# Block 1 attention: zero-padded tail operands, matmuls ordered by shape, five wide mark pairs on VectorE, new beat tables

## The reference, cut to what matters

```python
# two blocks on x of 32 sequences x 256 tokens x 128 features; after each part x = layernorm(x + part(x))
x = ln(x + state_space_mixer(x)); x = ln(x + ffn(x))          # block 0
# block 1, attention with 16 heads of 64, 4 memory keys in front of the 256 keys:
q, k, v = x @ Wq, x @ Wk, x @ Wv            # split by head; mem_k, mem_v put in front of k, v
dots = einsum('bhid,bhjd->bhij', l2norm(q), l2norm(k)) * 10
dots = einsum('hg,bgij->bhij', W_pre_th, dots)        # heads mixed before
dots = where(causal, mask_value, dots)
dots = where(dots < top_k(dots, 64)[0][..., -1:], mask_value, dots)
attn = einsum('hg,bgij->bhij', W_post_th, softmax(dots))   # heads mixed back
out = (attn @ v * head_scale) * sigmoid(x @ Wg + bg) @ Wo
x = ln(x + out); x = ln(x + ffn(x))
```

## Time and profile before

| | us |
|---|---|
| median of 3 runs (lowest, highest) | 4013.77 (4002.79, 4021.79) |
| the profiled execution's own time | 4020.4 |
| its span, first to last instruction | 4019.1 |
| mean granted TensorE clock in it | 0.953 of full |
| PE, DVE, ACT, POOL busy | 3641.7, 3418.9, 3097.5, 2068.1 |

### The profile page before, as it was taken

How to read it: one execution, slowest core, us unless ns; L and a number is a source line. 1 busy time by engine, 2 the same in 40 slices (tenths; PEclk the granted TensorE clock), 3 DMA queues, 4 the chain that set the end, 5 groups by cost and what they waited for, 6 DMA issues and landing times.

```text
span 4019.1 us, 78953 instructions
## 1 busy us (share of the span) xinstructions
PE 3641.7 (91%) x19551; PEld 2621.6 (65%) x19551; DVE 3418.9 (85%) x18221; ACT 3097.5 (77%) x10773; POOL 2068.1 (51%) x3991
## 2 busy tenths in 40 slices
PE   5999999986899998999999999999999999999987
PEld 3888888863666666666666666666666666666665
DVE  6888888835998888998999989988888889898894
ACT  5777777755788888888888888888888888888863
POOL 0000000014666667676666766666666766676664
PEclk7999999996999999999999999999999999999998
DMA  3000000001111111111111111111111111111110
GB/s 120 12 11 12 11 12 11 9 9 35 25 27 27 31 30 31 31 27 27 27 28 27 27 27 30 29 26 27 27 30 31 31 30 28 26 27 28 25 25 4
DMA packets 168123, 106.00 MB, mean 26 GB/s; under 512 B 78000, under 2 KB 165104, under 8 KB 166896
## 3 DMA queue, kind: packets, MB, share of 16 engines
q1 hardware_dynamic: 167664, 100.96, 11.7%
HBM read 20.70 MB, written 8.91 MB: 7 GB/s over the span
## 4 chain that ended last, share of the span: by engine, by line
POOL 29%; PE 27%; ACT 25%; issue 10%; DVE 7%; SPq 1%; DMA 1%; POOLq 0%; DVEq 0%; ACTq 0%
POOL below L1849 10%; PE bank L362 6%; POOL T L1859 6%; ACT T L1494 4%; ACT L1463 4%; POOL below L1851 3%; PE bank L330 3%; PE bank L1335 3%; POOL gate L1870 3%; ACT SN L1507 3%; POOL posts L1811 2%; ACT gate L1549 2%; DVE y L895 2%; PE bank L1356 2%; PE bank L431 1%
## 5 line engine op out<-in xcount | busy, mean ns | idle before, releaser
L1714 DVE MATCH_REPLACE8 W<-last,W 128x130 f32<-128x130 f32 (+17 forms) x3456 | 871.5, 259 | 0.0
L1735 DVE MAX8 last<-W 128x8 f32<-128x130 f32 (+17 forms) x3456 | 761.0, 261 | 0.0
L1849 POOL TENSOR_SCALAR below<-T,last 128x260 f32<-128x260 f32 (+8 forms) x576 | 597.7, 1038 | 176.6 <-DVE last L1733 126.2
L1494 ACT ACTIVATE T<-T,peak 128x260 f32<-128x260 f32 (+15 forms) x1024 | 418.1, 422 | 168.0 <-POOL T L1859 159.0
L1811 POOL TENSOR_SCALAR posts<-post,share 128x128 f32<-128x128 f32 x1024 | 376.2, 387 | 246.1 <-DVE share L1644 239.0
L1325 PE MATMUL bank<-T,pre 128*128 128x40 f32 (+15 forms) x1024 | 377.6, 452 | 126.0 <-ACT T L1515 103.5
L1335 PE MATMUL bank<-posts,T 128*128 128x128 f32 (+7 forms) x2048 | 412.2, 307 | 61.2 <-ACT AT L1532 57.8
L885 DVE TENSOR_TENSOR_SCAN hs<-dA,dx 128x256 f32<-128x256 f32 x512 | 349.5, 683 | 134.0 <-issue 100.7
L1507 ACT ACTIVATE SN<-bank,rq 128x260 f32<-128x260 f32 (+1 forms) x1024 | 360.7, 433 | 98.1 <-DMA T<-SN 46.2
L1335 PEld LDWEIGHTS bank<-posts,T 128*128 128x128 f32 (+7 forms) x2048 | 302.5, 182 | 182.7 <-POOL posts L1811 104.2
L521 POOL TENSOR_SCALAR k_sq<-k_sq 128x16 f32<-128x16 f32 x64 | 19.5, 305 | 707.0 <-DVE k_sq L534 572.4
(11 more groups left out here) (242 smaller groups left out, 9503.1 us busy)
## 6 DMA issues: line engine op xcount, KB each, us to landing
T<-SN SPq DMA_DIRECT2D x32, 130.0 KB
x_in<-in_xT SPq DMA_DIRECT2D x32, 128.0 KB, 2.2
x_mid<-x_b SPq DMA_DIRECT2D x32, 128.0 KB, 1.7
xb<-x_mid SPq DMA_DIRECT2D x32, 128.0 KB, 2.1
out_y<-x_d SPq DMA_DIRECT2D x32, 128.0 KB, 3.4
T<-SN SPq DMA_DIRECT2D x32, 126.0 KB
T<-SN SPq DMA_DIRECT2D x32, 122.0 KB
T<-SN SPq DMA_DIRECT2D x32, 118.0 KB
```

The costliest lines, as they stand in the source:

```text
L1494: act.activation(one, one, ACT.Exp, bias=peak[k % 2][:, j:j + 1], accum_out=total[k % 4][:, j:j + 1]).then_inc(e_made, 1)
L1714: dve.match_replace(both[:, s, at:to], best[n], both[:, s, at:to], LOWEST).then_inc(ranked, 1)
L1735: dve.max(best[n], both[:, s, at:to]).then_inc(ranked, 1)
L1849: pool.tensor_scalar(out[:, s, :], x[:, s, :], best[:, 7:8], DROP, ALU.is_lt, ALU.mult).then_inc(marked, 1)
```

## The change

1. `V2` and `AT2` get 128 partitions instead of 4. `V2` is filled with zeros once, `AT2` as before; data still goes to the first four. The matmuls of the last four tokens in `attend` now have 128 rows instead of 4.
2. `mix_back` does a whole quad at once: it waits for all four `posts`, and issues the matmuls in an order in which those of like shape stand together.
3. `CUT` names the wide pairs of quads 0, 2, 4, 6 and 7. Their marks are written by DVE at the end of `wide`; POOL only adds them. The other four wide pairs (those of quads 1, 3 and 5, and the 132-wide one of quad 7) and the narrow ones stay with POOL.
4. All beat tables have new numbers.

```diff
-    V, V2 = room.sb("V", [P, 2, INNER]), room.sb("V2", [MEM, INNER])
+    V, V2 = room.sb("V", [P, 2, INNER]), room.sb("V2", [P, INNER])
-    AT2 = room.sb("AT2", [MEM, HEADS, QG])
+    AT2 = room.sb("AT2", [P, HEADS, QG])
+    CUT = [[0], [], [0], [], [0], [], [0], [0]]
-    PE_MIX = (64, 71, 87, 94, 107, 110, 119, 123)
+    PE_MIX = (56, 71, 89, 96, 121, 125, 126, 129)
-    DVE_SHARE = (40, 66, 80, 84, 108, 111, 120, 135)
+    DVE_SHARE = (65, 83, 85, 98, 114, 117, 124, 136)
...
-        def mix_back(b, i, j):
+        def mix_back(b, i):
...
-            pe.wait_ge(posts_made, n + 1)
+            pe.wait_ge(posts_made, n + 4)
...
+            order = [(first, 0), (first, 1)]
+            if width(QUAD[i][2]) <= P // 2:
+                order += [(second, 0), (second, 1), (first, 2), (first, 3)]
+            else:
+                order += [(first, 2), (first, 3), (second, 0), (second, 1)]
+            for one, j in order:
+                last = one(j)
...
+            if j0 in CUT[i]:
+                out = mark_of(g, j0)
+                dve.wait_ge(found_wide, 2 * ((QUADS + 1) * b + i + j0 // 2 + 1))
+                if drops(k, DROPS[i][0]) > 1:
+                    dve.wait_ge(dropped, drops(k, DROPS[i][0]) - 1)
+                for n, (j, s) in enumerate(rows):
+                    dve.tensor_scalar(out[:, s, :], x[:, s, :], best[n][:, 7:8], DROP, ALU.is_lt, ALU.mult).then_inc(cut_marked, 1)
+                    yield
...
+                if j0 in CUT[i]:
+                    made.append((x, out, cut_marked, 2 * cuts(k, j0)))
+                    continue
```

More of the change, by code:

```diff
@@ L1147, in rank_steps, with cuts, mark_of @@
         return n
+    def cuts(k, j):
+        b, i = divmod(k, QUADS)
+        return CUT_ALL * b + sum(len(c) for c in CUT[:i]) + sum(x <= j for x in CUT[i])
+    def mark_of(g, j0):
+        return below[j0 // 2][:, 0:2 * width(g)].rearrange("p (two n) -> p two n", two=2)
     def drops(k, j):
@@ L1171, in attention_phase @@
[L1171 to L1185, removed]
@@ L1215, in attention_phase @@
-    ACT_K_SCALE = (13, 34)
-    POOL_K_CLIP = (1, 24)
-    POOL_K_ROOT = (11, 25)
+    PE_K = (-7, -6, 3, 3)
+    PE_K_TURN = (1, 2, 11, 24)
+    PE_Q = (11, 20, 23, 33)
+    PE_Q_SUM = (26, 30, 35, 36)
+    PE_Q_TURN = 44
+    PE_ATTEND = (5, 8, 8, 18)
+    PE_GATES = (34, 37, 39, 40)
+    PE_MIX = (56, 71, 89, 96, 121, 125, 126, 129)
+    PE_OUT = 25
+    PE_VAR1 = 33
+    PE_SPREAD1 = 38
+    PE_W1 = 41
+    PE_W2 = 45
+    PE_H1 = (63, 67, 67, 69)
+    PE_H2 = (79, 80, 91, 93)
+    PE_SCORE0 = (55, 60, 63)
@@ new lines, in attention_phase @@
+    PE_W3 = 94
+    PE_SCORE1 = (89, 91, 93, 95, 96, 100, 105, 107)
+    PE_VAR2 = 98
+    PE_SPREAD2 = 109
+    PE_V = (123, 127, 128, 128)
+    PE_PREMIX = [[71, 83, 89, 93, 104, 105, 118, 123], [125, 125, 128, 131, 136, 148, 164, 197]]
+    ACT_K = (-33, -24, 17, 21)
+    ACT_K_TURN = (9, 27, 30, 38)
+    ACT_Q = (30, 42, 43, 43)
+    ACT_K_ROOT = (-16, 24)
+    ACT_Q_SUM = 48
+    ACT_Q_ROOT = 55
+    ACT_PEAK = (-8, 33, 38, 42, 70, 78, 92, 114)
+    ACT_WIDE = (34, 39, 56, 69, 70, 80, 98, 123)
@@ L1219, in ctx_of @@
+    ACT_K_SCALE = (3, 28)
+    POOL_K_CLIP = (-21, 10)
+    POOL_K_ROOT = (-14, 12)
     def ctx_of(c2):
@@ L1410, in tensor @@
                 for i in range(QUADS):
-                    for j in range(4):
-                        if (b := whose(p, t, PE_MIX[i])) is not None:
-                            mix_back(b, i, j)
+                    if (b := whose(p, t, PE_MIX[i])) is not None:
+                        mix_back(b, i)
                 if (b := whose(p, t, PE_OUT, 2)) is not None:
@@ L1533, in at_keep @@
             if i == 0:
-                act.activation(AT2[:], turn(at1[0:MEM, 2 * P:3 * P]), ACT.Copy).then_inc(at_kept, 1)
+                act.activation(AT2[0:MEM, :, :], turn(at1[0:MEM, 2 * P:3 * P]), ACT.Copy).then_inc(at_kept, 1)
             if i == QUADS - 1:
@@ L1855, in drop @@
                 marks += 2
-                made.append((x, out, marks))
-            for x, out, n in made:
-                pool.wait_ge(marked, n)
+                made.append((x, out, marked, marks))
+            for x, out, ready, n in made:
+                pool.wait_ge(ready, n)
                 pool.tensor_tensor(x, x, out, ALU.add).then_inc(dropped, 1)
```

105 lines of the change are left out of this document (48 added, 57 removed).

## The result

| | before | changed |
|---|---|---|
| time, median | 4017.78 us (4 runs, 4002.79 to 4025.67) | 3849.31 us (4 runs, 3845.96 to 3863.54) |
| ratio, with its 95% interval | | 0.9592 (0.9554 to 0.963) |
| profiled execution, its span | 4020.4, 4019.1 us | 3863.54, 3862.2 us |

The sign was right; the size was not.

The account below looks back on a forecast made before the run. No engine was full; POOL's latency was what was waited for. DVE 3.5 us busier and 5.5 less idle gave -2.0 us a sequence, times 32 -64: 4020.4 to 3956, 3950 us on the median's scale; range 3870 to 4040.

Parts of the forecast that it names:

- What bounds the kernel, and the waits: Block 1: no engine full, POOL's latency waited for; DVE would wait 5.5 us less a sequence.
- the share's wait: DVE's wait for exponentials before its share, 4.4 us a sequence, of which 3.6 would go.
- the mask's: DVE's wait for POOL's causal mask before pairings of quads 0 and 2, 3.3 us a sequence; 1.9 would go.
- x_d's: DVE's wait for x_d from PE, 1.3 us a sequence, expected to stay.
- The marks' own price: Ten marks a sequence moved from POOL to DVE, 0.26 us each, 2.6 us of DVE's time.
- One cost is less sure: DVE's new marks colliding with POOL's gate products: 0.7 us a sequence more on DVE, ends 0 and 11.
- I count nothing of it directly: PE loses 3.2 of 87.1 busy us a sequence, counted as no direct gain since PE is idle 7.4 us.
- My count of the changes: PE's mix_back: eight fewer changes of weight columns in quads 5 to 7, none fewer elsewhere; 1.4 us a sequence.
- All of it pays: First rival, 16%: one collision of 1.1 us goes and the share never waits; -3.9 us a sequence, 3889 us.
- The wait moves: Second rival, 14%: later shares delay posts, mixing back and attend; PE or the output path becomes late; 4014 us.
- The port: Third rival, 18%: POOL's work holds each DVE mark 0.6 us; +3.3 us a sequence, 4120 us.

Follow-up runs that it names:

- experiment 12: The changed kernel with a semaphore for each pair's two regrouping DMAs instead of one for four: 3773.2 us, 0.9395 of the kernel before.
- experiment 7: The changed kernel with CUT empty, so all marks are on POOL again: 3931.2 us, 0.9785 of the kernel before.
- experiment 11: The changed kernel with all nine wide pairs marked by DVE: 3924.9 us, 0.9775 of the kernel before.
- experiment 8: The changed kernel with V2, AT2 and mix_back as before, so only new beats and DVE's marks: 3934.0 us, 0.9787 of the kernel before.
- Experiment 4: The kernel before with V2 and AT2 at 128 partitions and the new mix_back, old beats, no marks on DVE: 4026.6 us, ratio 1.0039.
- experiments 2 and 3: The changed kernel with the old beat tables (0.9957 of the kernel before); the kernel before with only the five pairs of marks on DVE (0.9958).
- experiment 5: The kernel before with each gate product as two one-input POOL instructions: 4008.2 us, ratio 0.9979.

## Why the prediction was wrong

**What bounds the kernel, and the waits: right in the main.** POOL's latency was on the path, and it left it (29% to 2%). I took 5.5 us of waits off DVE; 4.4 went (idle from 9.5 to 5.1). Of the share's wait 2.6 went (forecast 3.6), of the mask's 0.4 (forecast 1.9), and all of x_d's 1.3, which I had left standing. Quad 2's mask wait went as argued, but quad 0's was not POOL's doing: experiment 12 shows that in the changed kernel it came from SP's DMAs, further up. I followed that wait only to the engine that the row names.

**The marks' own price: right.** 0.29 to 0.43 us each by their records, median 0.323, a little over my 0.20 to 0.30; those of one quad overlap, and together they take 2.4 us a sequence of DVE's time (forecast 2.6, range 2.0 to 3.5).

**"One cost is less sure", the collisions: the term that failed in the sum.** I had +0.7 us, which my own words do not give (10 marks, 3 in 36, half as often again, 1.1 us: 1.4); the pairings took 2.7 less. The four pairings of the 228-wide pair are at 0.39 to 0.40 us; two of them had taken 1.3 on average. So DVE's busy time moved by -0.4 instead of +3.5, and that is more than the whole difference between a sequence of 92.5 and one of 89.7 us. I had the row, and had written that quad 2 was the one hit, with its mask moved ahead of the products in the order; only in the first rival did I draw the conclusion, and there I took one collision of 1.1 us for a loss of 2.4 in that quad. With the same tables the pairings take 11.7 us in experiment 7 and 12.8 in experiment 11, so that they meet nothing is a matter of this combination, and I had not foreseen it. What brings it is neither part alone: pairings take 11.8 us with the beats, 12.4 with the marks, 10.3 with both (experiment 8).

**"I count nothing of it directly", PE: the step that failed as a mechanism.** The busy time fell from 87.3 to 83.7, 3.6 us for 3.2; by the estimate above 2.8 of it are work and the rest is the clock. But with marks and beats in place, leaving PE's relief out makes a sequence 1.7 us longer by experiment 8's profile (91.4 against 89.7), and 2.6 by the medians (85 us, 2.0%). I put the direct gain at nothing because I read 7.4 us of idle PE as room. I even wrote that without the relief PE would stand at 94%; at 95% it carried 54% of the chain. With the old order the shapes gained nothing (1.0039), so a trial of them there would have misled. My count of the changes was off and its cost was not: in quads 1 to 4 the columns change less often too (four times before, twice now), but changes between 128 and 68 columns cost next to nothing (quad 4, 1.32 us for twelve instructions), and from 128 to 52, 36 or 20 they cost some 0.2 us.

**The rivals.** "All of it pays" came nearest, 3889 us against 3849, in part by luck: it named the collision, but the share, which was never to wait, still waits for 1.8 us. Its plea held better than its sum: the four engines lost 14.3 of 313.8 busy us, 4.6%, and the sequence 5.1%. What I held against it was misread, since with one collision less DVE would be at 87.3 of 90.6 us (96%), and it came to 84.6 of 89.7 (94%). "The wait moves" did not happen in the changed kernel. Experiment 4 looks like it in small, for the old beats: four posts to wait for and no gain, though the clock had its part there. "The port" did not happen in the changed kernel: a mark took 0.323 us at the median and 0.426 at most, against 0.286 for the mixer's one-input instruction of 256 columns, and the mean of 260 columns was 0.354; a hold of 0.27 on each was its condition. But its mechanism is real, and only the order spares the marks. By the Trainium skill (GPSIMD Engine Reference, Key points) marks in a 2-port mode would be exposed like the pairings. The trace of experiment 12 agrees that they are exposed: eight of its marks of 228 columns start inside a gate product and end with it, after 1.09 to 1.26 us for 0.34. One of them, in the timeline, and all marks of that run (ns min/median/max):

```profile
2263.56 1.27 POOL L1906 TENSOR_TENSOR gate<-gate,f_b 128x512 f32<-128x512 f32 x1
2263.71 1.51 DVE L1768 TENSOR_SCALAR below<-T,last 128x228 f32<-128x228 f32 x2 [1.32 <-POOL T L1895]
...
L1768 DVE TENSOR_SCALAR below<-T,last x286: 280/321/1258, 1206.1 to 3677.9; 128x260 f32<-128x260 f32 x29, 128x228 f32<-128x228 f32 x29, 128x196 f32<-128x196 f32 x29, 128x164 f32<-128x164 f32 x28
```

With the old beats (experiments 2 and 3) one of the two marks of 196 columns starts inside POOL's one-input `open_gate` of 512 columns and takes 0.57 to 0.60 us for 0.32.

## What to carry to other kernels

- Price two reliefs together, not each against the old profile. Where several engines are at 90% and more of the period, each one alone is hidden behind the others; POOL's marks and PE's shapes brought 0.5% each and 2.4% together. Ask what the period would be with each engine's relief withheld in turn.
- An order of work has a price in how instructions meet, not only in who waits. Look for instructions of one shape whose mean is two or three times their free duration (1282 ns for 390), and ask whether the new order still has them meet their neighbour; count that as a term, with the sign.
- Follow a wait up until the chain ends in something that has no wait before it. DVE waited for POOL, POOL for ACT, ACT for PE, PE for a DMA that was one of sixteen in a queue; a finer semaphore there was worth 2.0% at no cost in work.
- Read the granted clock beside PE's busy time. The same matmuls took 83.7 us of PE in the changed kernel and 81.6 in experiment 12, with the clock at half for 4.5 and for 1.4 us; a wait of PE may cost more than its own length.

## What the runs showed of the hardware

- Two-input instructions of DVE and POOL that begin together do not share: the DVE one of 228 columns took 1.48 us beside POOL's of 1.27, 0.39 free. The neighbour need not be the gate product: in experiment 7 a 244-wide pairing averages 1.18 us for 0.41 beside POOL's 520-wide addition, and in experiment 11 quad 0's take 1.0 us for 0.43 beside 296-wide ones. One-input instructions of POOL with constants hold a pairing too, for less: 0.80 us in experiment 5, about twice the free time. A one-input mark of DVE can be held as a pairing is (1.26 us for 0.34 in experiment 12). POOL's own marks hold nothing: in the kernel before, 29 pairings of 244 columns that started with 1.35 us left of a mark of 260 columns took 0.41, their free time.
- On PE a change of the weights' columns (128 to 52 and back) cost 0.21 us: two fewer in quad 5 took 2.03 to 1.60 us. Between 128 and 68 columns it cost next to nothing: quad 4, in which they alternate before the change, takes 1.32 us for twelve instructions, 0.11 each. The four-row weights between 128-row ones cost 0.25 us a group of `attend`, 1.03 to 0.78, although the zeros put 124 empty rows into each load.
- SP issued a regrouping DMA every 0.65 us (0.61 and 0.04 between), fifteen in 9.8 us, against 3.3 us from the last one's issue to its landing: here the issue queue, more than the transfer, set when the last one arrived.
- The TensorE clock stood at its half level for 1.4 to 8.8 us of a sequence. There 128 columns of `mix_back` took 213 ns instead of 112. In experiment 8 it fell after PE had worked for 0.10 of 2 us.
